# Where the numerator of the time mixing is made: VectorE behind the reciprocal, or GpSimd beside the denominator

## The chip, the cores and the metric

The kernel runs on one core of a Trainium2 chip. It is a single program that computes two transformer layers. The metric is its time on the device in microseconds. The kernel before takes 920.26 us, the median of 3 runs (918.15 to 921.51).

## The reference

There are 8 x 256 tokens of 256 features. Layer 0 is attention followed by a mixture of four experts, layer 1 is an RWKV time mixing followed by a mixture of eight experts. The change lies in the time mixing. Its core is a recurrence over the 256 tokens of a sequence, for each feature apart:

```
def step(carry, kv):
    aa, bb, pp = carry
    kt, vt = kv
    qt = jnp.maximum(pp, kt + u)
    e1 = jnp.exp(pp - qt)
    e2 = jnp.exp(kt + u - qt)
    out = (e1 * aa + e2 * vt) / (e1 * bb + e2)
    pp_new = jnp.maximum(pp + neg_ew, kt)
    f1 = jnp.exp(pp - pp_new)
    f2 = jnp.exp(kt - pp_new)
    return ((f1 * aa + f2 * vt, f1 * bb + f2, pp_new), out)
```

Around it: `k`, `v` and `r` are projections of the token mixed with the one before it, and the output is `r` times the layer norm of `out`, projected by `Wo` and added to the residual:

```
wkv = _wkv(time_decay, time_first, k, v)
mu = jnp.mean(wkv, axis=-1, keepdims=True)
var = jnp.mean(jnp.square(wkv - mu), axis=-1, keepdims=True)
ln = (wkv - mu) * jax.lax.rsqrt(var + LN_EPS) * ln_g + ln_b
rwkv = r * ln
return jnp.einsum('btd,ed->bte', rwkv, Wo)
```

## The kernel before, in words

The program is a chain of phases with a barrier between each two. The time mixing (`rwkv_phase`) is one of them. It makes eight passes, one per sequence `b` of 256 tokens. Features lie on the partitions, in two blocks of 128, and tokens lie along a row, so that almost every elementwise operation is 128 partitions by 512 elements of float32, all in SBUF unless a PSUM bank is named.

Each engine runs through the same hand-written list, `schedule(w)`, and does only the steps that it has; its instructions run in the order of that list. Semaphores, one per kind of result, order the engines among each other: `done["wkv_done"]` counts the passes whose `wkv` is there. Inside an engine an instruction that reads what the one ahead has written waits for its semaphore as well; in `divide` the small helper `then` does both. Several steps of the pass before, `b - 1`, lie between the steps of pass `b`.

The steps of one pass, with the engine and the line:

- `scores`: VectorE makes the running maximum (two scans, L1665), `less` (L1669); ScalarE takes the exponentials (L1631); GpSimd multiplies by `v` (`grow`, L1759). `gap`: VectorE, L1675. `clamp`: ScalarE makes `ex`, which holds e1 and e2 (L1640), GpSimd makes `e2v` (L1763).
- `vary(b - 1)`: TensorE's variance matmuls (L1572), VectorE's small addition (L1716), GpSimd's inverse root (L1768).
- `scan`: VectorE makes `ab`, the sums aa and bb, with four scans of 128x256 (L1682). On GpSimd `scan` is the numerator: e1 times aa (`e1a`, L1772), and its sum with `e2v` (`num`, L1776).
- `gather_up(b + 3)`: GpSimd adds the two expert outputs of a later sequence to the residual (L1743, L1746), after ScalarE has weighed them (`weigh`, L1586). Only the first five passes have it.
- `divide`: VectorE makes the denominator (L1694, L1695), its reciprocal (L1696) and the product with `num` (`wkv`, L1699).
- `add(b - 1)` and `stats(b + 3)` on VectorE; then, in the next pass of the list, `centre(b)` on TensorE (L1545), `square` on ScalarE (L1626), `gate` on VectorE (L1706), `shift`, `add_shift` (L1711) and `project` (L1563).

`products(b + 1)` on TensorE (L1533, 48 matmuls) lies beside `scan` and `divide`.

Of the kernel before, what the change touches and what calls it, by code (L numbers as in the profile page):

```python
# [7 lines left out]
ALU = mybir.AluOpType  # L8
# [6 lines left out]
B, T, D = 8, 256, 256  # L15
# [15 lines left out]
def at_least(eng, semaphore, value):  # L31

    if not (isinstance(value, int) and value <= 0):
        eng.wait_ge(semaphore, value)
# [1361 lines left out]
def rwkv_phase(nc, m, r, k, ctx):  # L1396
# [13 lines left out]
    less, sc, ab = sb("less", [P, 2, EB, T]), sb("sc", [P, 3, EB, T]), sb("ab", [P, 2, EB, T + 1])  # L1410
    dif, rel, ex = sb("dif", [P, EB, T]), sb("rel", [P, 2, EB, T]), sb("ex", [P, 2, EB, T])
    e2v, e1a, num, den, rden, wkv, sq, rw = (
        sb(n, [P, EB, T]) for n in ("e2v", "e1a", "num", "den", "rden", "wkv", "sq", "rw"))
# [6 lines left out]
    done = {n: sem(n) for n in names.split()}  # L1420
# [6 lines left out]
    def schedule(w):  # L1427

        def front(b):
            w.turn(b)  # L1430
            w.take_x(b)

        for b in range(2):
            w.weigh(b)
            w.gather_up(b)
            w.stats(b)
            w.root(b)
            w.norm(b)
            if b == 0:
                front(0)  # L1440
        w.products(0)
        w.weigh(2)
        w.gather_up(2)
        w.stats(2)
        for b in range(B):
            if b + 1 < B:
                front(b + 1)
            if b > 0:
                w.centre(b - 1)
            w.scores(b)  # L1450
            if b > 0:
                w.square(b - 1)
            w.grow(b)
            if b + 2 < B:
                w.root(b + 2)
            w.gap(b)
            if b > 0:
                w.gate(b - 1)
                w.shift(b - 1)
            w.clamp(b)  # L1460
            if b > 0:
                w.add_shift(b - 1)
                w.project(b - 1)
                w.vary(b - 1)
            if b + 2 < B:
                w.norm(b + 2)
            if b + 3 < B:
                w.weigh(b + 3)
            if b + 1 < B:
                w.products(b + 1)  # L1470
            w.scan(b)
            if b + 3 < B:
                w.gather_up(b + 3)
            w.divide(b)
            if b > 0:
                w.add(b - 1)
            if b + 3 < B:
                w.stats(b + 3)
        for step in (w.centre, w.square, w.gate, w.shift, w.add_shift, w.project, w.vary, w.add):
            step(B - 1)  # L1480
# [27 lines left out]
    @block.sync  # L1508
    def _(sp):
        for b in range(B):  # L1510
            for c in range(2):
                plane = k.y_dram[c * TOK + S * P * b:c * TOK + S * P * (b + 1)]
                sp.dma_start(y[:, c, S * b:S * b + S, :], plane.rearrange("(s p) d -> p s d", p=P)).then_inc(here[c][b], 16)
# [132 lines left out]
    def _(dve):  # L1646
        class Dve(Work):
# [38 lines left out]
            def divide(self, b):  # L1686
                def then(ins, name):

                    ins.then_inc(done[name], 1)
                    dve.wait_ge(done[name], b + 1)  # L1690

                dve.wait_ge(done["scan_done"], b + 1)
                dve.wait_ge(done["ex_done"], b + 1)
                then(dve.tensor_tensor(den[:], ex[:, 0], ab[:, 1, :, 0:T], ALU.mult), "e1b_done")  # L1694
                then(dve.tensor_tensor(den[:], den[:], ex[:, 1], ALU.add), "den_done")  # L1695
                then(dve.reciprocal(rden[:], den[:]), "rden_done")  # L1696
                dve.wait_ge(done["num_done"], b + 1)
                at_least(dve, done["centred"], b)
                dve.tensor_tensor(wkv[:], num[:], rden[:], ALU.mult).then_inc(done["wkv_done"], 1)  # L1699

# [36 lines left out]
    @block.gpsimd  # L1737
    def _(pool):
        class Pool(Work):
            def gather_up(self, b):  # L1740
                two = m.x_res[:, S * b:S * b + S, :]
                pool.wait_ge(done["first_weighed"], b + 1)
                pool.tensor_tensor(two, two, y[:, 0, S * b:S * b + S, :], ALU.add).then_inc(done["first_added"], 1)  # L1743
                pool.wait_ge(done["first_added"], b + 1)
                pool.wait_ge(done["second_weighed"], b + 1)
                pool.tensor_tensor(two, two, y[:, 1, S * b:S * b + S, :], ALU.add).then_inc(done["added"], 1)  # L1746

            def root(self, b):
                two = slice(S * b, S * b + S)
                pool.wait_ge(done["ve_in_done"], b + 1)  # L1750
                pool.tensor_tensor(m.rstd[:, two], ve_in[:, two], m.neg_half[:, 0:S], ALU.pow).then_inc(done["root_done"], 1)
                pool.wait_ge(done["root_done"], b + 1)
                pool.tensor_tensor(neg_mean[:, two], less_mean[:, two], m.rstd[:, two], ALU.mult).then_inc(done["neg_mean_ready"], 1)

            def grow(self, b):
                pool.wait_ge(done["sc_done"], b + 1)
                pool.wait_ge(done["v_ready"], b + 1)
                at_least(pool, done["scan_done"], b)
                pool.tensor_tensor(sc[:, 0], sc[:, 1], vs[:], ALU.mult).then_inc(done["f2v_done"], 1)  # L1759

            def clamp(self, b):
                pool.wait_ge(done["ex_done"], b + 1)
                pool.tensor_tensor(e2v[:], ex[:, 1], vs[:], ALU.mult).then_inc(done["e2v_done"], 1)  # L1763

            def vary(self, b):
                pool.wait_ge(done["ve_done"], b + 1)
                at_least(pool, done["x_done"], b)
                pool.tensor_tensor(rstd[:], ve[:], m.neg_half[:, 0:S], ALU.pow).then_inc(done["rstd_done"], 1)  # L1768

            def scan(self, b):  # L1770
                pool.wait_ge(done["scan_done"], b + 1)
                pool.tensor_tensor(e1a[:], ex[:, 0], ab[:, 0, :, 0:T], ALU.mult).then_inc(done["e1a_done"], 1)  # L1772
                pool.wait_ge(done["e1a_done"], b + 1)
                pool.wait_ge(done["e2v_done"], b + 1)
                at_least(pool, done["wkv_done"], b)
                pool.tensor_tensor(num[:], e1a[:], e2v[:], ALU.add).then_inc(done["num_done"], 1)  # L1776

        pool.memset(xt[:, :, :, 0], 0.0)
        pool.memset(top[:, :, 0], NEVER)
        pool.memset(ab[:, :, :, 0], 0.0).then_inc(done["edges"], 1)  # L1780
        schedule(Pool())
        pool.wait_ge(done["eps_done"], 1)
        pool.tensor_tensor(m.rstd[:], m.var_eps[:], m.neg_half[:, 0:NT], ALU.pow).then_inc(done["next_rstd"], 1)
# [86 lines left out]
```

## Time and profile before

| | |
|---|---|
| median of 3 runs | 920.26 us (918.15 to 921.51) |
| profiled execution | 921.07 us |
| its span | 919.3 us |
| busy: TensorE, VectorE | 666.3 us (72%), 541.0 us (59%) |
| busy: ScalarE, GpSimd | 354.4 us (39%), 287.9 us (31%) |
| mean granted TensorE clock | 0.871 of full speed |
| VectorE reciprocals, L1696 | 8, mean 3353 ns |
| VectorE second denominator step, L1695 | 8, mean 1552 ns |
| GpSimd L1772 and L1776 | 8 each, mean 1685 and 1596 ns |

The profile is of one execution. PE is TensorE, PEld its weight loads, DVE VectorE, ACT ScalarE, POOL GpSimd, SP the queue that starts transfers. A row of the timeline gives the start from the beginning of the span, the length, the engine, the line and operation, what it writes and reads, and in brackets how long the engine was idle ahead of it and what released it. The row of a line that occurs several times in a row is merged, with the count at its end. Busy shares over the whole span mix phases of different kinds, so that the stretch of the time mixing has to be read by itself.

### The profile page before, as it was taken

What the parts mean: (1) busy time and instruction counts of PE and PEld (TensorE: products, weight loads), DVE (VectorE), ACT (ScalarE), POOL (GpSimd) and SP (SyncE); (2) the same over time, 40 slices, a digit from 0 to 9 for tenths busy, and PEclk for the clock granted to TensorE, in tenths of its full rate; (3) what the DMA queues carried; (4) which work ended last, traced back from release to release, by engine and by line L of the source; (5) the groups of instructions that cost most, each with busy time, mean ns of one, the idle gap of its engine ahead of it and who ended that gap; (6) DMA issues with size and microseconds to landing.
All of it is one profiled execution on the core that took longest, in us unless ns stands there. A gap on an engine that the chain in (4) does not pass through costs nothing. (4 is left out here: it accounts for less than half of the span.)

```text
span 919.3 us, 14453 instructions
## 1 busy us (share of the span) xinstructions
PE 666.3 (72%) x4496; PEld 560.0 (61%) x4496; DVE 541.0 (59%) x1117; ACT 354.4 (39%) x782; POOL 287.9 (31%) x265
## 2 busy tenths in 40 slices
PE   0389999846971999999963798999507439999800
PEld 0266666526971788888853677888407428888700
DVE  3138787843976455554431588888657755555433
ACT  0048777722531233333323545644104314444300
POOL 3134324010001334433323454552330033332075
PEclk9989999986995899999995989999755559999955
DMA  3000000003520211111105000000025313323144
GB/s 103 16 1 2 2 1 2 2 5 134 183 81 7 86 58 54 57 52 59 52 30 184 0 1 0 1 0 1 0 73 173 125 35 92 93 93 87 53 132 142
DMA packets 38311, 52.20 MB, mean 57 GB/s; under 512 B 7222, under 2 KB 30392, under 8 KB 38232
## 3 DMA queue, kind: packets, MB, share of 16 engines
q1 hardware_dynamic: 31468, 32.74, 11.1%
q0 software_dynamic: 6768, 18.49, 7.0%
q8 instruction: 43, 0.70, 0.3%
q14 instruction: 32, 0.26, 0.1%
HBM read 35.22 MB, written 15.99 MB: 56 GB/s over the span
## 5 line engine op out<-in xcount | busy, mean ns | idle before, releaser
L1533 PE MATMUL banks<-r_xt,r_w_mixed 128*128 128x256 f32 x384 | 86.6, 385 | 3.0 <-ACT r_xt L1601 3.0
L1533 PEld LDWEIGHTS banks<-r_xt,r_w_mixed 128*128 128x128 f32 x384 | 73.2, 192 | 14.0 <-ACT r_xt L1601 3.6
L1299 DVE SCALAR_TENSOR_TENSOR f0x_s<-f0x_th,banks 128x512 f32<-128x512 f32 x35 | 24.1, 689 | 83.3 <-ACT f0x_th L1267 80.8
L614 POOL TENSOR_TENSOR a_rr<-a_ms_eps,neg_half 128x32 f32<-128x32 f32 x8 | 44.0, 5503 | 89.6 <-DVE a_ms_eps L507 89.6
L1176 POOL DMA_INDIRECT f_y<-f0x_yout,f_slot_of x35 | 34.4, 983 | 103.1 <-ACT f0x_yout L1280 101.0
L1162 POOL DMA_INDIRECT f1x_xg<-f_xn,f_token_of x39 | 37.0, 948 | 80.9 <-PE banks L1213 55.4
L1229 PE MATMUL banks<-f_w_hi,f0x_xt_hi 128*128 x140 | 58.9, 420 | 0.2 <-issue 0.2
L534 DVE TENSOR_REDUCE a_ssum<-a_e 128x6 f32<-128x1536 f32 x32 | 55.7, 1742 | 2.3 <-ACT a_e L466 2.3
L1229 PE MATMUL banks<-f_w_lo,f0x_xt_hi 128*128 x140 | 56.0, 400 | 0.0
L1229 PE MATMUL banks<-f_w_hi,f0x_xt_lo 128*128 x140 | 55.6, 397 | 0.0
L1267 ACT ACTIVATE f0x_th<-banks 128x512 f32<-128x512 f32 x35 | 21.0, 599 | 83.8 <-PE banks L1229 83.8
L466 ACT ACTIVATE a_e<-banks 128x1536 f32<-128x1536 f32 x32 | 46.5, 1454 | 12.8 <-PE banks L368 12.8
L1162 POOL DMA_INDIRECT f0x_xg<-f_xn,f_token_of x35 | 33.9, 968 | 30.7 <-POOLq L1809 20.3
L368 PE MATMUL banks<-a_ut,a_qt 32*128 32x256 f32 x512 | 37.6, 408 | 7.8 <-ACT a_e L456 5.6
L1299 DVE SCALAR_TENSOR_TENSOR f1x_s<-f1x_th,banks 128x256 f32<-128x256 f32 x39 | 16.4, 421 | 45.0 <-ACT f1x_th L1267 44.3
L1250 PE MATMUL banks<-f_w_hi,f0x_ht_hi 128*128 x140 | 42.4, 303 | 0.7 <-ACT f0x_yout L1280 0.7
L1356 POOL DMA_INDIRECT f1c_y<-f_y,f_row_of x32 | 30.3, 946 | 38.7 <-PEq L1806 29.3
L1250 PE MATMUL banks<-f_w_lo,f0x_ht_hi 128*128 x140 | 39.5, 282 | 0.0
L1250 PE MATMUL banks<-f_w_hi,f0x_ht_lo 128*128 x140 | 39.4, 281 | 0.0
L393 PE MATMUL banks<-a_e,a_vv 128*32 128x256 f32 x512 | 34.3, 385 | 3.4 <-DVE a_vv L549 2.7
L368 PEld LDWEIGHTS banks<-a_ut,a_qt 32*128 32x128 f32 x512 | 24.0, 188 | 19.6 <-issue 12.9
L1366 DVE SCALAR_TENSOR_TENSOR x_res<-f1c_y,f_weight,x_res 128x256 f32<-128x256 f32 x32 | 15.5, 484 | 32.5 <-DMA f1c_y<-f_y,f_row_of 30.3
(362 smaller groups left out, 2034.1 us busy)
## 6 DMA issues: line engine op xcount, KB each, us to landing
f_y<-f1x_yout SPq DMA_DIRECT2D x39, 128.0 KB, 1.7
f0r_stage<-in_f_w13T SPq DMA_DIRECT2D x4, 1024.0 KB
r_y<-f_y SPq DMA_DIRECT2D x16, 256.0 KB, 5.7
f1r_stage<-in_f_w13T SPq DMA_DIRECT2D x8, 512.0 KB, 5.3
x_res<-in_L_attn_x SPq DMA_DIRECT2D x2, 1024.0 KB
f0r_stage<-in_f_w2T SPq DMA_DIRECT2D x4, 512.0 KB
f_xn<-f0r_xn SPq DMA_DIRECT2D x8, 256.0 KB
f1r_stage<-in_f_w2T SPq DMA_DIRECT2D x8, 256.0 KB, 5.4
```

The costliest lines, as they stand in the source:

```text
L368: last = pe.matmul(scores[:, i, s, :], qt[rows, b % 2, e, k, s * P:(s + 1) * P], ut[rows, b % 2, k, :], start=True, stop=True)
L393: last = pe.matmul(av(n)[32 * i:32 * i + 32, :], values[:, b % 2, head, :, :].rearrange("p r d -> p (r d)"), side[:, S * i + s, :], start= ...
L466: act.activation(ebuf[:, n % 3, 0:SUMS_ON_DVE, :], scores[:, 0:SUMS_ON_DVE // S].rearrange("p i s t -> p (i s) t"), ACT.Exp).then_inc(exp_ ...
L534: dve.tensor_reduce(ssum[:, b % 2, NB * p:NB * p + SUMS_ON_DVE], ebuf[:, n % 3, 0:SUMS_ON_DVE, :], AX_X, ALU.add).then_inc(sum_done, 1)
L614: pool.tensor_tensor(rr[:], ms_eps[:], m.neg_half[:, 0:S * NH], ALU.pow).then_inc(rr_found, 1)
L1162: pool.indirect_dma_start(xg[:, t % GB, :], None, k.xn_dram, bass.IndirectOffsetOnAxis(ap=k.token_of[:, t:t + 1], axis=0)).then_inc(gather ...
L1176: pool.indirect_dma_start(k.y_dram, bass.IndirectOffsetOnAxis(ap=k.slot_of[:, t:t + 1], axis=0), yout[:, t % YB, :], None).then_inc(scatte ...
L1229: last = pe.matmul(out, xt[a][:, t % 2, kb * P:(kb + 1) * P], k.w13[c][kb][:, e, cols], start=(i == 0 and not v.lin_bias), stop=(i == len( ...
L1250: last = pe.matmul(y_psum, ht[a][:, t % 2, hb * P:(hb + 1) * P], k.w2[c][hb][:, e, :], start=(i == 0 and not v.lin_bias), stop=(i == len(s ...
L1299: dve.scalar_tensor_tensor(out=s1[:, t % 2, :], in0=th[:, t % 2, :], scalar=1.0, in1=glu(t), op0=ALU.add, op1=ALU.mult).then_inc(s1_done, 1)
L1356: pool.indirect_dma_start(y[:, t % GB, c, :], None, k.y_dram, bass.IndirectOffsetOnAxis(ap=k.row_of[:, c * NT + t:c * NT + t + 1], axis=0) ...
L1533: last = pe.matmul(bank(1 + kind)[:, eb * T:(eb + 1) * T], r.w_mixed[:, kind, j // KB, j % KB, eb * P:(eb + 1) * P], xt[:, b % 2, j % KB, ...
```

## The change

VectorE makes the numerator itself. In `divide`, behind the reciprocal, two instructions are added: `e1a` = e1 times aa, and `num` = `e1a` + `e2v`. The wait for `num_done` becomes a wait for `e2v_done`. GpSimd's `scan` step is taken away with its two instructions and its waits. The semaphores keep their names and counts.

```diff
--- before.py
+++ after.py
@@ -1694,7 +1694,9 @@
                 then(dve.tensor_tensor(den[:], ex[:, 0], ab[:, 1, :, 0:T], ALU.mult), "e1b_done")
                 then(dve.tensor_tensor(den[:], den[:], ex[:, 1], ALU.add), "den_done")
                 then(dve.reciprocal(rden[:], den[:]), "rden_done")
-                dve.wait_ge(done["num_done"], b + 1)
+                then(dve.tensor_tensor(e1a[:], ex[:, 0], ab[:, 0, :, 0:T], ALU.mult), "e1a_done")
+                dve.wait_ge(done["e2v_done"], b + 1)
+                then(dve.tensor_tensor(num[:], e1a[:], e2v[:], ALU.add), "num_done")
                 at_least(dve, done["centred"], b)
                 dve.tensor_tensor(wkv[:], num[:], rden[:], ALU.mult).then_inc(done["wkv_done"], 1)
 
@@ -1767,13 +1769,6 @@
                 at_least(pool, done["x_done"], b)
                 pool.tensor_tensor(rstd[:], ve[:], m.neg_half[:, 0:S], ALU.pow).then_inc(done["rstd_done"], 1)
 
-            def scan(self, b):
-                pool.wait_ge(done["scan_done"], b + 1)
-                pool.tensor_tensor(e1a[:], ex[:, 0], ab[:, 0, :, 0:T], ALU.mult).then_inc(done["e1a_done"], 1)
-                pool.wait_ge(done["e1a_done"], b + 1)
-                pool.wait_ge(done["e2v_done"], b + 1)
-                at_least(pool, done["wkv_done"], b)
-                pool.tensor_tensor(num[:], e1a[:], e2v[:], ALU.add).then_inc(done["num_done"], 1)
 
         pool.memset(xt[:, :, :, 0], 0.0)
         pool.memset(top[:, :, 0], NEVER)
```

On VectorE, the second pass, from the four scans of `scan` (L1682, called SCALAR_TENSOR_TENSOR here and TENSOR_TENSOR_SCAN in the trace) to `add` (`x_res`, and its BN_STATS). `r_ex` holds e1 and e2, `r_ab` aa and bb. Before:

```order
L1682 SCALAR_TENSOR_TENSOR r_ab<-r_sc 128x256 x4
L1694 TENSOR_TENSOR r_den<-r_ex,r_ab 128x512
L1695 TENSOR_TENSOR r_den<-r_den,r_ex 128x512
L1696 RECIPROCAL r_rden<-r_den 128x512
L1699 TENSOR_TENSOR r_wkv<-r_num,r_rden 128x512
L1724 SCALAR_TENSOR_TENSOR x_res<-banks,r_rstd,x_res 128x256 x2
L1729 BN_STATS bn<-x_res 128x6 x2
```

After:

```order
L1682 SCALAR_TENSOR_TENSOR r_ab<-r_sc 128x256 x4
L1694 TENSOR_TENSOR r_den<-r_ex,r_ab 128x512
L1695 TENSOR_TENSOR r_den<-r_den,r_ex 128x512
L1696 RECIPROCAL r_rden<-r_den 128x512
L1697 TENSOR_TENSOR r_e1a<-r_ex,r_ab 128x512
L1699 TENSOR_TENSOR r_num<-r_e1a,r_e2v 128x512
L1701 TENSOR_TENSOR r_wkv<-r_num,r_rden 128x512
L1726 SCALAR_TENSOR_TENSOR x_res<-banks,r_rstd,x_res 128x256 x2
L1731 BN_STATS bn<-x_res 128x6 x2
```

Two instructions of 128x512 stand between the reciprocal and the product with it; everything behind them in the queue is two places later.

On GpSimd, from `r_e2v` of the second pass to `grow` (`r_sc`) of the third and the root for a later norm (`rstd`). The root of the variance is L1768 before and L1770 after, the two additions of the gather are L1743 and L1746 before, L1745 and L1748 after. Before:

```order
L1763 TENSOR_TENSOR r_e2v<-r_ex,r_vs 128x512
L1768 TENSOR_TENSOR r_rstd<-r_ve,neg_half 128x2
L1772 TENSOR_TENSOR r_e1a<-r_ex,r_ab 128x512
L1776 TENSOR_TENSOR r_num<-r_e1a,r_e2v 128x512
L1743 TENSOR_TENSOR x_res<-x_res,r_y 128x512
L1746 TENSOR_TENSOR x_res<-x_res,r_y 128x512
L1759 TENSOR_TENSOR r_sc<-r_sc,r_vs 128x512
L1751 TENSOR_TENSOR rstd<-r_ve_in,neg_half 128x2
```

After:

```order
L1765 TENSOR_TENSOR r_e2v<-r_ex,r_vs 128x512
L1770 TENSOR_TENSOR r_rstd<-r_ve,neg_half 128x2
L1745 TENSOR_TENSOR x_res<-x_res,r_y 128x512
L1748 TENSOR_TENSOR x_res<-x_res,r_y 128x512
L1761 TENSOR_TENSOR r_sc<-r_sc,r_vs 128x512
L1753 TENSOR_TENSOR rstd<-r_ve_in,neg_half 128x2
L1755 TENSOR_TENSOR r_neg_mean<-r_less_mean,rstd 128x2
```

The two additions of the gather move up: they follow the root of the variance directly.

## Rows read from the trace of the kernel before

The columns of rows 1 and 6 are: the stretch, its length, then busy time and number of instructions of PE, PEld, DVE, ACT and POOL (of PE alone in rows 6), the granted TensorE clock as a part of full speed, the busy share of the DMA engines, and GB/s.

**Rows 1.** Busy time by stretch, the first and the third pass; columns named above.

```profile
520.00:539.00 19.00, 12.42 (x52) 10.40 (x50) 15.40 (x20) 11.58 (x21) 12.02 (x12) 0.82 0.00 0
...
557.90:576.60 18.70, 17.18 (x85) 14.87 (x85) 16.15 (x26) 10.09 (x19) 10.20 (x10) 1.00 0.01 1
```

**Rows 2.** Waits from 515 to 675 us: total, times, longest.

```profile
DVE r_ve L1716 <- PE banks L1572: 17.3, 8, 2.3
...
PE banks L1545 <- DVE r_wkv L1699: 15.9, 2, 9.3
...
DVE r_rw L1706 <- PE banks L1545: 3.0, 1, 3.0
```

**Rows 3.** Timeline of the third pass, all engines: start, length, instruction, idle before.

```profile
557.71 10.62 PE L1533 MATMUL banks<-r_xt,r_w_mixed 128*128 128x256 f32 x48
557.89 0.16 DVE L1716 TENSOR_SCALAR r_ve<-banks 128x2 f32<-128x2 f32 x1 [2.28 <-PE banks L1572]
557.97 2.74 DVE L1682 TENSOR_TENSOR_SCAN r_ab<-r_sc 128x256 f32<-128x256 f32 x4
558.22 1.69 ACT L1586 ACTIVATE r_y<-r_y,f_weight 128x256 f32<-128x256 f32 x4
558.37 1.07 POOL L1768 TENSOR_TENSOR r_rstd<-r_ve,neg_half 128x2 f32<-128x2 f32 x1
560.74 0.69 DVE L1694 TENSOR_TENSOR r_den<-r_ex,r_ab 128x512 f32<-128x512 f32 x1
560.78 1.69 POOL L1772 TENSOR_TENSOR r_e1a<-r_ex,r_ab 128x512 f32<-128x512 f32 x1 [1.33 <-DVE r_ab L1682]
...
561.46 1.55 DVE L1695 TENSOR_TENSOR r_den<-r_den,r_ex 128x512 f32<-128x512 f32 x1
...
562.55 1.60 POOL L1776 TENSOR_TENSOR r_num<-r_e1a,r_e2v 128x512 f32<-128x512 f32 x1
563.05 3.35 DVE L1696 RECIPROCAL r_rden<-r_den 128x512 f32<-128x512 f32 x1
564.11 1.27 POOL L1743 TENSOR_TENSOR x_res<-x_res,r_y 128x512 f32<-128x512 f32 x1
...
565.45 1.27 POOL L1746 TENSOR_TENSOR x_res<-x_res,r_y 128x512 f32<-128x512 f32 x1
566.44 0.83 DVE L1699 TENSOR_TENSOR r_wkv<-r_num,r_rden 128x512 f32<-128x512 f32 x1
...
568.61 0.60 PE L1545 MATMUL banks<-r_wkv,r_cen_same 128*128 128x256 f32 x2
...
570.54 0.60 ACT L1626 ACTIVATE r_sq<-banks 128x512 f32<-128x512 f32 x1 [1.08 <-PE banks L1545]
...
573.01 0.68 DVE L1706 TENSOR_TENSOR r_rw<-banks,r_s 128x512 f32<-128x512 f32 x1
...
573.75 1.99 PE L1563 MATMUL banks<-r_wo_gain,r_rw 128*128 128x256 f32 x8 [1.52 <-DVE r_rw L1706]
...
576.56 0.16 DVE L1716 TENSOR_SCALAR r_ve<-banks 128x2 f32<-128x2 f32 x1 [2.28 <-PE banks L1572]
```

**Rows 4.** Timeline of the first pass.

```profile
520.79 3.46 DVE L1682 TENSOR_TENSOR_SCAN r_ab<-r_sc 128x256 f32<-128x256 f32 x4 [1.88 <-POOL r_sc L1759]
...
522.01 1.70 POOL L1763 TENSOR_TENSOR r_e2v<-r_ex,r_vs 128x512 f32<-128x512 f32 x1
```

**Rows 5.** Single lines: ns least/median/most, first and last start.

```profile
L1682 DVE TENSOR_TENSOR_SCAN r_ab<-r_sc x32: 656/659/1691, 520.8 to 650.7; 128x256 f32<-128x256 f32 x32
...
L1694 DVE TENSOR_TENSOR r_den<-r_ex,r_ab x8: 691/692/693, 524.3 to 651.3; 128x512 f32<-128x512 f32 x8
...
L1695 DVE TENSOR_TENSOR r_den<-r_den,r_ex x8: 1549/1552/1555, 525.0 to 652.1; 128x512 f32<-128x512 f32 x8
...
L1699 DVE TENSOR_TENSOR r_wkv<-r_num,r_rden x8: 691/816/836, 530.0 to 657.0; 128x512 f32<-128x512 f32 x8
```

**Rows 6.** Busy time by stretch, TensorE alone, in the attention phase.

```profile
172.00:184.00 12.00, 9.89 (x126) 1.00 0.00 1
```

## The prediction

> **What bounds the kernel now.** Only one of the kernel's phases is touched, the time mixing, whose eight passes over pairs of 128-token tiles fill about 520 to 670 us. I first read the busy time by stretch, one stretch per pass. In the third pass VectorE is busy for 16.15 of 18.70 us and TensorE for 17.18, so either could be the bound, and the shares do not say which [rows 1]. The waits of the phase do. VectorE has one wait that returns in every pass: 17.3 us in 8 times, at most 2.3 each, at the small addition that starts a pass (L1716), for TensorE's variance matmuls (L1572) [rows 2]. The timeline of the third pass closes the loop. VectorE starts L1716 at 557.89 and has no other wait until the gate product L1706 ends at 573.69 (573.01 + 0.68); TensorE, which had stood 1.52 us for exactly that product, starts the projection at 573.75, its variance matmuls follow, and VectorE goes on with the next L1716 at 576.56 [rows 3]. The period of 18.67 us is thus 15.8 us of VectorE's queue plus 2.87 us of TensorE behind it. Everything that lengthens VectorE's queue lengthens the pass by as much. TensorE starts the centring (L1545) only at 568.61, though its input r_wkv is there from 567.27 (566.44 + 0.83): it has 1.3 us in hand at that place and another 1.52 before the projection [rows 3]. In the first and the last pass it has nothing in hand: two waits of 15.9 us together for r_wkv, and the last pass's gate waits 3.0 us for the centring [rows 2]. So the result of the division is on the path in all eight passes: through VectorE's own queue in the first seven, through TensorE's wait in the last.
>
> GpSimd's decayed product and sum (L1772, L1776) are not on it. The sum ends at 564.15 (562.55 + 1.60), inside the reciprocal, which runs from 563.05 to 566.40 [rows 3]. What they cost today is interference. L1695 adds two SBUF tensors of the same size as L1694 and takes 1549 to 1555 ns in all 8 passes, against 691 to 693 for L1694 [rows 5]; the difference of 0.86 us stands where GpSimd's L1772 is running, itself 1.69 us long where the same kind of operation in L1743 takes 1.27 [rows 3]. L1699, too, takes 0.83 us while L1746 is still running until 566.72 and a least 0.69 us elsewhere [rows 3, 5]. So an operation of either engine with two SBUF inputs is held up until the other's is through. The reciprocal, with one input, shows no such thing: 3.35 us with two and a half GpSimd operations beside it [rows 3].
>
> **The change part by part.**
>
> *Added on VectorE.* Two 128x512 products per pass, behind the reciprocal and each waited for before the next goes. The first is L1694's form, the second L1695's. The pitch from L1694 to L1695, the wait for completion included, is 561.46 - 560.74 = 0.72 us [rows 3]. 8 x 2 x 0.72 = +11.5 us, all on the path. The wait for e2v in front of the sum costs nothing: e2v is GpSimd's operation before L1768, which starts at 558.37 [rows 3], and the sum comes eight microseconds later.
>
> *Removed: the interference with L1695 and L1699.* If nothing took the place of GpSimd's two operations, L1695 would fall to 0.69: 8 x 0.86 = -6.9 us. L1699 would be 0.69 in all passes; it is longer by 0.12 to 0.14 in the five passes that still gather (median 816, least 691) [rows 5]: 5 x 0.14 = -0.7 us.
>
> *Moved: the gathers.* GpSimd's queue is in order, and with the two operations gone its next ones after the root L1768 are the two additions of the gather for three passes on (L1743, L1746), in the first five passes. Today they run from 564.11 to 566.72, under the reciprocal, where they meet only the start of L1699. After the change they wait for nothing but ScalarE's weighing L1586: four instructions in the 1.69 us from 558.22, the first two done by about 559.1 [rows 3]. L1768 ends at 559.45, so L1743 starts at about 559.50, amid VectorE's four scans (557.97 to 560.71), which also read two SBUF inputs. What such a meeting costs is seen in the first pass: GpSimd's L1763 starts at 522.01 within the four scans and takes 1.70 instead of 1.27, and the four scans take 3.46 us [rows 4]; the longest scan of all is 1691 ns where the median is 659 [rows 5]. The meeting costs VectorE 1.03 us. By the same steps L1743 is held until about 559.9, ends at 561.2 and puts the last scan off by 1.03. L1746 then starts at about 561.3 behind the last scan's reads and stands before L1694, which it puts off by as much again. I take 1.03 for both, the row nearest to what they meet: 5 x 2 x 1.03 = +10.3 us. The bounds of one meeting are 0 (they happen to fall between VectorE's operations) and 1.27 (the whole of L1743): 0 to 12.7 in all. L1695, after them, is free in all eight passes, as counted.
>
> By the Trainium skill ("SBUF — State Buffer", section "Who interferes with whom") whoever comes first has the shared ports for the whole instruction and the other stops entirely, which would make a meeting worth up to the whole gather addition; with 1.27 for 1.03 the sum would be 2.4 us more. The 1.03 us of [rows 5] is below that, and I keep the row's value.
>
> *Sum.* 11.5 - 6.9 - 0.7 + 10.3 = +14.2 us: about +2.5 in each of the first five passes, +0.58 (1.44 - 0.86) in each of the last three. The profiled execution took 921.07 us, of which 919.3 are span; it would go to 935.3. It lies 0.8 above the median of 920.26, to which I add the same 14.2: **934.5 us**.
>
> *What is late next.* With r_wkv 2.5 us later in the middle passes, TensorE's 1.3 us in hand at the centring is gone and it starts 1.2 us later. The squares (L1626) that follow start at 570.54, and the gate that wants them at 573.01, itself 2.5 later: they stay ahead [rows 3]. TensorE then idles about 4 of 21.2 us per pass.
>
> **The rivals.**
>
> *A. The gathers hit less than I say.* They are put off by ScalarE or slip between two operations, so that about one meeting per pass is paid instead of two: 14.2 - 5.2 = +9.0, 929.3 us. For it: the start at 559.50 lies within about 0.1 us of the third scan's own start, if the scans (0.66 us each, four in 2.74) start some 0.6 us apart, so small shifts change who goes first. Against it: GpSimd's 2.6 us of gathers starting at 559.5 cannot avoid the stretch to 562 in which VectorE reads two tensors almost without pause. If both meetings were free, 14.2 - 10.3 = +3.9, 924.2 us; this needs the order of GpSimd's queue not to matter at all.
>
> *B. TensorE's clock falls.* With more idle time per pass, the granted clock, now 1.00 in the third pass and 0.82 in the first, where TensorE stood for r_wkv [rows 1, 2], could drop to the lower level for part of a pass. In the first pass TensorE is busy 12.42 of 19 us. If the projection and the variance behind it (2.87 us) ran at 1.2 GHz instead of 2.4, that is up to +2.9 us per pass for seven passes, +20: 954 us, and the products, 10.62 us at full clock [rows 3], would come near to bounding the pass. Against it: at 172 to 184 us it is busy 9.89 of 12.00, 82%, with the clock at 1.00 [rows 6], and the pass after the change would have 17.2 of 21.2, 81%.
>
> *C. Not slower: the loop closes through TensorE.* If TensorE, with 17.18 of 18.70 us busy, set the pass, then six of eight passes would swallow VectorE's additions up to the 1.3 us in hand at L1545 and the 1.52 at L1563, and only the first and last pass would pay: +2.5 + 0.6 = +3.1 at most, 923.3 us, or nothing if the earlier gathers help the next norm. It decides if VectorE's addition is under what TensorE has in hand and the 2.3 us wait at L1716 shrinks by it. Against it: that wait is behind TensorE's wait for L1706, so it cannot shrink when L1706 comes later.
>
> **How the numbers follow.** The forecast (both meetings paid, loop through VectorE) 0.63; A 0.15 for one meeting and 0.09 for none; B 0.07; C 0.04, with another 0.02 for a gain that I have no mechanism for. The likeliest case is 934.5. The range reaches down to A's first case and up past the dearer meeting, 927 to 940, leaving out B and the cases of 924 and less. What a measurement of this kernel can tell from no change is about 0.5%, 4.6 us, so 924.9 is the line of slower. Slower: 0.63 + 0.15 + 0.07 and a little of A's second case, 0.86; within 0.5%: the rest of A and C, 0.12; faster 0.02.
>
> **What would show it.** Right: L1695 at 0.69 in all passes; the two new VectorE lines at 0.69 each with a pitch of 0.72; a last scan of about 1.7 us and an L1694 of about 1.7 us in five passes, with the gather additions beside them; a period of about 21.2 us in passes two to five and 17.9 in six and seven; VectorE's wait at L1716 still 2.3 us; TensorE waiting more for r_wkv. Wrong: gathers that still run beside the reciprocal or scans of 0.66 throughout (A); a granted clock under 1.00 in passes two to seven (B); a shrinking wait before the variance addition (C).

## The result and the profile after

The changed kernel takes 937.38 us, the median of 4 runs (936.2 to 938.35), against 919.88 us for the kernel before, also of 4. The ratio is 1.019, with a 95% interval of 1.0168 to 1.0212: slower by 17.5 us where +14.2 was forecast, and inside the range. The profiled execution has a span of 936.6 us and a mean granted clock of 0.858.

The same view as in [rows 1], from one small variance addition (L1718, L1716 before) to the next: the stretch, its length, busy time of PE, PEld, DVE, ACT and POOL, granted clock, DMA share, GB/s.

```profile
541.30:564.37 23.07, 19.02 (x85) 16.19 (x85) 18.84 (x27) 11.86 (x24) 7.88 (x8) 0.92 0.00 1
...
585.10:606.37 21.27, 17.41 (x85) 14.87 (x85) 18.65 (x27) 10.08 (x19) 7.17 (x8) 1.00 0.00 0
606.37:629.30 22.93, 19.08 (x85) 16.22 (x85) 18.66 (x28) 10.51 (x19) 7.71 (x8) 0.92 0.00 1
```

The fourth pass, between 585 and 606, is as forecast: 21.27 us long with the clock at 1.00, against 18.70 in [rows 1]. The two others shown, the second and the fifth, are 1.8 and 1.7 us longer still, at a clock of 0.92. The fourth pass in the timeline (start, length, instruction, idle before), to be read against [rows 3]:

```profile
585.10 0.16 DVE L1718 TENSOR_SCALAR r_ve<-banks 128x2 f32<-128x2 f32 x1 [2.28 <-PE banks L1572]
585.18 4.89 DVE L1682 TENSOR_TENSOR_SCAN r_ab<-r_sc 128x256 f32<-128x256 f32 x4
...
585.59 1.08 POOL L1770 TENSOR_TENSOR r_rstd<-r_ve,neg_half 128x2 f32<-128x2 f32 x1
586.64 1.27 POOL L1745 TENSOR_TENSOR x_res<-x_res,r_y 128x512 f32<-128x512 f32 x1
587.99 1.53 POOL L1748 TENSOR_TENSOR x_res<-x_res,r_y 128x512 f32<-128x512 f32 x1
...
590.10 0.69 DVE L1694 TENSOR_TENSOR r_den<-r_ex,r_ab 128x512 f32<-128x512 f32 x1
590.83 0.69 DVE L1695 TENSOR_TENSOR r_den<-r_den,r_ex 128x512 f32<-128x512 f32 x1
591.55 3.35 DVE L1696 RECIPROCAL r_rden<-r_den 128x512 f32<-128x512 f32 x1
...
594.94 0.69 DVE L1697 TENSOR_TENSOR r_e1a<-r_ex,r_ab 128x512 f32<-128x512 f32 x1
...
595.66 0.69 DVE L1699 TENSOR_TENSOR r_num<-r_e1a,r_e2v 128x512 f32<-128x512 f32 x1
...
596.39 0.69 DVE L1701 TENSOR_TENSOR r_wkv<-r_num,r_rden 128x512 f32<-128x512 f32 x1
...
597.14 0.70 PE L1545 MATMUL banks<-r_wkv,r_cen_same 128*128 128x256 f32 x2 [1.16 <-DVE r_wkv L1701]
...
602.82 0.68 DVE L1708 TENSOR_TENSOR r_rw<-banks,r_s 128x512 f32<-128x512 f32 x1
...
603.56 1.99 PE L1563 MATMUL banks<-r_wo_gain,r_rw 128*128 128x256 f32 x8 [2.70 <-DVE r_rw L1708]
...
606.37 0.16 DVE L1718 TENSOR_SCALAR r_ve<-banks 128x2 f32<-128x2 f32 x1 [2.28 <-PE banks L1572]
```

The numerator's product and sum stand behind the reciprocal with pitches of 0.72 and 0.73 us. L1695 takes 0.69 us where it took 1.55. The gather additions L1745 and L1748 run at 586.64 and 587.99, amid the scans, and the four scans take 4.89 us instead of 2.74. VectorE has no wait from L1718 to the gate product L1708; TensorE stands 1.16 us for r_wkv and 2.70 for L1708, which it did for 0 and 1.52 before. VectorE's own wait is again 2.28.

The single lines over all passes, as in [rows 5] (ns least, median, most):

```profile
L1682 DVE TENSOR_TENSOR_SCAN r_ab<-r_sc x32: 656/680/1775, 520.8 to 668.2; 128x256 f32<-128x256 f32 x32
...
L1694 DVE TENSOR_TENSOR r_den<-r_ex,r_ab x8: 691/692/1583, 524.3 to 668.8; 128x512 f32<-128x512 f32 x8
...
L1695 DVE TENSOR_TENSOR r_den<-r_den,r_ex x8: 691/692/1640, 525.9 to 669.6; 128x512 f32<-128x512 f32 x8
...
L1748 POOL TENSOR_TENSOR x_res<-x_res,r_y x8: 1254/1531/1592, 490.1 to 609.3; 128x512 f32<-128x512 f32 x8
```

L1694 is long in the first and the third pass and L1695 in the first; in the second, fourth and fifth both gather additions fall among the scans. The waits of the phase, as in [rows 2] (total, times, longest):

```profile
PE banks L1545 <- DVE r_wkv L1701: 20.8, 5, 9.9
DVE r_ve L1718 <- PE banks L1572: 20.1, 8, 3.9
...
PE banks L1563 <- DVE r_rw L1708: 11.4, 5, 2.7
```

VectorE waits 20.1 us instead of 17.3 for the variance, at most 3.9. The pass that ends with the 3.89 us shows why:

```profile
553.53 0.70 PE L1545 MATMUL banks<-r_wkv,r_cen_same 128*128 128x256 f32 x2 [1.35 <-DVE r_wkv L1701]
...
559.95 2.89 PE L1563 MATMUL banks<-r_wo_gain,r_rw 128*128 128x256 f32 x8 [2.70 <-DVE r_rw L1708]
...
562.63 1.70 PE L1572 MATMUL banks<-r_mean_of,r_sq 128*128 128x1 f32 x8
...
564.37 0.16 DVE L1718 TENSOR_SCALAR r_ve<-banks 128x2 f32<-128x2 f32 x1 [3.89 <-PE banks L1572]
564.45 3.46 DVE L1682 TENSOR_TENSOR_SCAN r_ab<-r_sc 128x256 f32<-128x256 f32 x4
...
565.60 1.76 POOL L1745 TENSOR_TENSOR x_res<-x_res,r_y 128x512 f32<-128x512 f32 x1
567.44 1.53 POOL L1748 TENSOR_TENSOR x_res<-x_res,r_y 128x512 f32<-128x512 f32 x1
567.95 1.57 DVE L1694 TENSOR_TENSOR r_den<-r_ex,r_ab 128x512 f32<-128x512 f32 x1
```

TensorE had stood for r_wkv and again for the gate product, and then took 2.89 us for a projection that takes 1.99, and 1.70 for variance matmuls that took 0.95 at full clock. By the profile the granted clock was 1.00 until 560 us and 0.50 from 561 to 567 us, the lower of its two levels (2.4 and 1.2 GHz). What TensorE did before it fell was to stand those 1.35 and 2.70 us.

### The profile page after: what moved, and what is told of

Same layout as the page of the kernel before. It is cut to its first block and busy times, and to the rows that moved or that the text cites. A ratio compares the mean times of both kernels' runs of the same rounds, so it can differ in the third digit from the quotient of the medians.

```text
span 936.6 us, 14452 instructions
## 1 busy us (share of the span) xinstructions
PE 676.3 (72%) x4496; PEld 567.6 (61%) x4496; DVE 555.3 (59%) x1133; ACT 354.1 (38%) x782; POOL 263.6 (28%) x249
## 5 line engine op out<-in xcount | busy, mean ns | idle before, releaser
L1533 PE MATMUL banks<-r_xt,r_w_mixed 128*128 128x256 f32 x384 | 93.0, 405 | 3.0 <-ACT r_xt L1601 3.0
L1533 PEld LDWEIGHTS banks<-r_xt,r_w_mixed 128*128 128x128 f32 x384 | 77.9, 205 | 15.8 <-ACT r_xt L1601 3.6
L1761 POOL TENSOR_TENSOR r_sc<-r_sc,r_vs 128x512 f32<-128x512 f32 x8 | 10.2, 1276 | 99.8 <-ACT r_sc L1631 99.8
```

The costliest lines, as they stand in the source:

```text
L1533: last = pe.matmul(bank(1 + kind)[:, eb * T:(eb + 1) * T], r.w_mixed[:, kind, j // KB, j % KB, eb * P:(eb + 1) * P], xt[:, b % 2, j % KB, ...
```

## The experiments

Where a kernel is compared with another than the one before, both ratios to the kernel before are used, since each group of runs had its own runs of that kernel (medians of 920.56 to 921.36 us).

**e1: the gathers back under the reciprocal**

```diff
     pool.wait_ge(done["first_weighed"], b + 1)
+    at_least(pool, done["den_done"], b - 2)
     pool.tensor_tensor(two, two, y[:, 0, S * b:S * b + S, :], ALU.add).then_inc(done["first_added"], 1)
```

> The changed kernel, with GpSimd's first gather addition (L1745 there) of the first five passes also waiting for the denominator of its pass, so that both additions run beside the reciprocal again, as before the change. Theory, that the moved gathers cost what they hold up in VectorE's scans and denominator (in the third pass of the changed kernel 3.46 - 2.74 us in the scans and 1.57 - 0.69 in L1694, 1.6 together; up to 2.5 in the second): five passes give back 8 to 10 us, 937.4 to about 928.5 (927 to 930), all scans near 0.66 us, L1694 and L1695 both at 0.69 in all eight passes. Rival 1, that only the two products added to VectorE count and the place of the gathers does not: no change, 937 (936 to 938.5). Rival 2, that the clock of TensorE is the larger part of what lies beyond 11.5 us: the gathers' delay gives back under 4 us, 933.5 or more.

Measured: 926.88 us, ratio 1.0059 (1.0043 to 1.0076). The place of the gathers alone is worth 1.019 - 1.0059 = 0.013, 12 us, somewhat more than the 8 to 10 expected. The two denominator lines, all eight passes:

```profile
L1694 DVE TENSOR_TENSOR r_den<-r_ex,r_ab x8: 692/692/692, 525.3 to 657.6; 128x512 f32<-128x512 f32 x8
...
L1695 DVE TENSOR_TENSOR r_den<-r_den,r_ex x8: 691/692/693, 526.0 to 658.4; 128x512 f32<-128x512 f32 x8
```

The terms that are left, 11.5 - 6.9 - 0.7 = +3.9, would give 1.0042. One wait for the variance in this trace is 4.0 us, 1.7 more than the usual 2.3; with it the sum is +5.6, and 0.0059 of 921.2 is 5.4. Rivals 1 and 2 are out. The expectation counted VectorE's lengths alone and left out the clock, and the changed kernel has two such long waits where e1 has one. That this is all of the 2 to 4 us by which it was missed is not shown.

**e8: only one of the two additions meets VectorE**

```diff
     pool.wait_ge(done["second_weighed"], b + 1)
+    at_least(pool, done["den_done"], b - 2)
     pool.tensor_tensor(two, two, y[:, 1, S * b:S * b + S, :], ALU.add).then_inc(done["added"], 1)
```

> The changed kernel, with only the second gather addition (L1748 there) waiting for the denominator, so that in the first five passes one of the two meets VectorE's scans and the other runs beside the reciprocal. Theory, that each meeting costs VectorE about 1 us: between e1 (none, 1.006 of before) and the changed kernel (both, 1.019), five us above e1: a ratio of 1.0115 (1.010 to 1.013), about 932. Rival, that only the pair costs, by making TensorE's clock fall: near e1, under 1.009, or near the changed kernel, over 1.016.

Measured: 932.64 us, ratio 1.0122 (1.0101 to 1.0143), halfway as expected. The third pass, and the end of it:

```profile
561.04 3.86 DVE L1682 TENSOR_TENSOR_SCAN r_ab<-r_sc 128x256 f32<-128x256 f32 x4
...
583.71 0.16 DVE L1718 TENSOR_SCALAR r_ve<-banks 128x2 f32<-128x2 f32 x1 [4.78 <-PE banks L1572]
```

The scans take 3.86 us, 1.1 more than the 2.74 of before. The clock takes part here too: the wait that ends this pass is 4.78 us, and the execution that was profiled is the slowest of the six (929.41 to 936.0 us). So the halfway ratio is not a clean price of one meeting; the length of the scans is.

**e2: the two operations alone, added to the kernel before**

The lines that declare the two tiles and their semaphores are left out here.

```diff
     then(dve.reciprocal(rden[:], den[:]), "rden_done")
+    then(dve.tensor_tensor(more1[:], ex[:, 0], ab[:, 0, :, 0:T], ALU.mult), "more1_done")
+    then(dve.tensor_tensor(more2[:], more1[:], ex[:, 1], ALU.add), "more2_done")
```

> The kernel before, with two further 128x512 operations of the same forms (e1 times aa, and a sum with e2) on VectorE behind the reciprocal, written to tiles that nobody reads; GpSimd makes the numerator as before. It measures the first term of the sum alone. Theory, that VectorE's queue sets the period of every pass: 8 x 2 x 0.72 = +11.5 us, 919.9 to 931.4 (930 to 934 with some clock loss), L1695 still at 1.55 us in all passes. Rival, that the loop closes through TensorE: at most +3.1, under 923.5.

Measured: 935.08 us, ratio 1.015 (1.0131 to 1.0169), or +13.9. The rival, a loop that closes through TensorE, is out. But 13.9 is 2.4 more than 11.5, and the product with the reciprocal, 0.69 us in every pass of this trace, should have given 0.7 back. The wait for the variance (total, times, longest) tells where a part of it lies, in the slowest of the five executions (939.0 us):

```profile
DVE r_ve L1719 <- PE banks L1573: 20.8, 8, 4.8
```

**e10: e2 with filler matmuls**

TensorE gets work that nobody reads in the place where it stands for the gate product, in passes two to six. The two operations of e2 are in it as well; their lines are left out here.

```diff
     last.then_inc(done["shifted"], 1)
+    if 1 <= b <= 5:
+        at_least(pe, done["ve_done"], b)
+        for n in range(4 if b < 5 else 3):
+            pe.matmul(bank(5)[:, T:2 * T], m.ident[:], r.wo_shift[:, n % EB, :], start=True, stop=True)
```

> The kernel of e2 (before, with two more 128x512 operations on VectorE per pass) with four filler matmuls behind the shift product of the second to the fifth pass, three in the sixth. Theory, that e2's excess over 11.5 us is TensorE's clock: no low stretch in passes two to six, VectorE's wait for the variance 2.3 at most, 11.5 - 0.7 = 10.8 us above before, a ratio of 1.012 (1.0105 to 1.0135) against e2's 1.015. Rival, that two more operations cost more than their own pitch elsewhere: the same 1.015.

Measured: 931.69 us, ratio 1.0115 (1.0094 to 1.0136), or +10.6. Doing more on TensorE made the kernel shorter by 0.0035; the two intervals overlap by a little (this one ends at 1.0136, e2's starts at 1.0131), so the ratios alone leave room, but the view agrees:

```profile
DVE r_ve L1723 <- PE banks L1577: 17.3, 8, 2.3
```

Total and longest are again those of [rows 2]. With the clock kept up, the first term less the 0.7 us of the product with the reciprocal, 10.8 us, is thus measured as 10.6.

**e4: eight fillers in every pass of the changed kernel**

The edit of e10, without the condition on `b` and with eight matmuls.

> The changed kernel, with eight matmuls of 128x256 by constants into an unused part of a PSUM bank behind the shift product of each pass, where TensorE stands 1.5 to 2.7 us for VectorE's gate product. They only keep TensorE busy. Theory, that about 3 us of the 17.5 come from the granted clock, which is at 0.5 for two stretches of 6.8 us in the third and the sixth pass and makes VectorE wait 3.9 instead of 2.3 us for the variance matmuls: no such stretch in passes two to seven, VectorE's wait 2.3 at most, 937.4 to about 934.5 (933 to 936). Rival, that these stretches come from elsewhere or cost nothing: 937 or more, slower still if the fillers (1.9 us at full clock) hold up the projection in the passes where the wait is shorter.

Measured: 946.67 us, ratio 1.0274 (1.0255 to 1.0293): slower than the changed kernel by 0.0073 to 0.0084, 7 to 8 us, against the theory's number and as its rival warned. The fillers were mis-sized: each is 0.43 us, eight take 3.45, not 1.9. In the pass after the last gather (TensorE alone):

```profile
644.25 3.62 PE L1559 MATMUL banks<-r_wo_shift,ident 128*128 128x256 f32 x16
647.70 1.89 PE L1566 MATMUL banks<-r_wo_gain,r_rw 128*128 128x256 f32 x8
```

The projection (L1566) starts right behind the fillers (L1559), with no idle time for the gate product. The four passes that begin at 545, 566, 588 and 609 us are nonetheless 21.23 us each, all alike, with the granted clock at 1.00, where the changed kernel has 23.07, 20.73, 21.27 and 22.93: 3.1 us less together. The loss lies in the first pass (4.4 us) and the last three (7.1 together), by the starts of the variance addition. The run shows that the low stretches go with TensorE's idle time, and does not price them.

**e6: four fillers in four passes**

The edit of e10 with `if 1 <= b <= 4` and four matmuls, on the changed kernel.

> The changed kernel, with four filler matmuls (0.43 us each by e4's trace, 1.7 together) instead of eight, and only behind the shift product of the second to the fifth pass, where TensorE stands 1.8 to 2.7 us for the gate product. Theory, that the low clock in the third and sixth pass costs about 3 us: the fillers fit into the wait, the clock stays at 1.00 there, VectorE's wait for the variance is 2.3 at most, 937.4 to about 934.5 (933 to 935.5). Rival 1, that the clock's share is nothing: 937 or more. Rival 2, that four do not keep it up: the same low stretches, 937 to 938.

Measured: 933.36 us, ratio 1.0138 (1.0121 to 1.0156). This interval lies clear of the changed kernel's in both of its measurements (1.019, and 1.0201 in e9). The third pass of e6 by stretch, columns as above, then its wait for the variance, and then the sixth pass of the changed kernel:

```profile
561.50:582.80 21.30, 19.17 (x93) 16.41 (x93) 18.68 (x28) 10.10 (x19) 7.20 (x8) 1.00 0.00 1
```

```profile
DVE r_ve L1722 <- PE banks L1576: 17.3, 8, 2.3
```

```profile
629.30:647.89 18.59, 18.59 (x85) 16.08 (x86) 15.25 (x22) 7.27 (x12) 2.81 (x3) 0.91 0.00 1
```

The clock is 1.00 in e6, the wait 2.3 at most. The clock is worth 0.0052 to 0.0063, 5 to 6 us; the theory's 3 was too low. It counted the two longer waits alone (3.89 and 3.93 instead of 2.28 us, 3.3 together). But the second low stretch reaches into the sixth pass, where TensorE is then busy for all of 18.59 us; the sixth and seventh pass take 18.59 and 18.15 us, against 17.94 and 17.88 in e6, 0.9 more. What is left, 0.0138 or 12.7 us, is the change without its clock loss: the meetings with the gathers, worked out as under "The moved gathers" below, cost VectorE 10.2 us here, as good as the changed kernel's 10.3.

**e7: the kernel before, again, and e9: the changed kernel, again**

> The kernel before once more, for a second trace. The traces of the changed kernel and of e1 to e3 have 13.6 us for the first 24 products of the time mixing, that of before 12.2, with the granted clock at 0.5 for 23.9 and 20.5 us around it. Theory, that this belongs to the single trace and not to the change: here 13.6 us too, or the low stretch placed otherwise, and the phase 1 to 1.5 us longer than 187.8; passes two to seven with the periods of the first trace (18.4 to 18.7 and 17.3) and the clock at 1.00. Rival, that it comes from the change: 12.2 us and 187.8 again.

Measured: 922.21 us, one run. The phase takes 190.4 us here, not 187.8, which is more than the 1 to 1.5 us expected, and the first 24 products, 48 records in the trace, take about as long as the 13.6 us in the changed kernel's trace:

```profile
497.27 13.67 PE L1533 MATMUL banks<-r_xt,r_w_mixed 128*128 128x256 f32 x48 [0.69 <-ACT r_xt L1601]
```

In the first trace they took 12.2 us. So what the opening of the phase takes differs by over a microsecond between two executions of one kernel, and a difference of that kind between the traces of before and after is not the change's. From the third pass on the periods are the first trace's within 0.01 us (18.67, 18.69, 18.68, 17.33, 17.29) with the clock at 1.00 in the passes of [rows 1]'s kind.

> The changed kernel once more, on the chip of the next run, so that the kernels of the study can be set against it, and for a second trace. Theory: a ratio of 1.017 to 1.021 to the kernel before; in the first five passes one or two operations of VectorE with two SBUF inputs longer by 0.7 to 1.1 us each for a gather addition; one to three stretches of the lower TensorE clock within passes two to seven, not all at the places of the first trace. Rival, that the two stretches are fixed by the program: again in the third and the sixth pass, 6.8 us each.

Measured: 939.29 us, ratio 1.0201 (1.0178 to 1.0223). The waits for the variance are again long at the start of the third and the sixth pass (3.84 and 3.85 us), and the scans again take 3.46 us in the third pass and 4.89 in the fourth and fifth. The rival expectation holds: the low stretches are where they were, within 0.5 us. The theory's guess that they would move did not come true.

**e3: the numerator stays on GpSimd, but under the reciprocal**

```diff
     pool.wait_ge(done["scan_done"], b + 1)
+    pool.wait_ge(done["den_done"], b + 1)
     pool.tensor_tensor(e1a[:], ex[:, 0], ab[:, 0, :, 0:T], ALU.mult).then_inc(done["e1a_done"], 1)
```

> The kernel before, with GpSimd's first numerator product (L1772 there) waiting for the finished denominator, so that both its operations run beside the reciprocal and not beside L1694 and L1695. Theory, that the interference of 0.86 us per pass at L1695 is a matter of place alone: L1695 falls to 0.69 in all passes, the numerator (2 x 1.34 us) is there before the reciprocal's 3.35 us are over, and the first gather addition, which then starts just ahead of the product with the reciprocal (L1699), holds that up by 0.2 to 0.5 in five passes: -6.9 + 1 to 2, 919.9 to about 914.5 (913 to 916). Rival, that the numerator comes too late or that the interference moves along with it: the same time or slower, 920 to 924.

Measured: 916.54 us, ratio 0.9949 (0.9932 to 0.9966). One more wait on the kernel before makes it faster, by 4.7 us, a little less than the 5 to 6 expected:

```profile
579.55 0.69 DVE L1695 TENSOR_TENSOR r_den<-r_den,r_ex 128x512 f32<-128x512 f32 x1
...
580.27 3.35 DVE L1696 RECIPROCAL r_rden<-r_den 128x512 f32<-128x512 f32 x1
580.38 1.18 POOL L1773 TENSOR_TENSOR r_e1a<-r_ex,r_ab 128x512 f32<-128x512 f32 x1 [2.85 <-DVE r_den L1695]
581.64 1.27 POOL L1777 TENSOR_TENSOR r_num<-r_e1a,r_e2v 128x512 f32<-128x512 f32 x1
582.87 1.27 POOL L1743 TENSOR_TENSOR x_res<-x_res,r_y 128x512 f32<-128x512 f32 x1
...
583.66 1.03 DVE L1699 TENSOR_TENSOR r_wkv<-r_num,r_rden 128x512 f32<-128x512 f32 x1
```

L1695 is free, both numerator operations end before the reciprocal does at 583.62, and the first gather addition holds L1699 up to 1.03 us, 0.2 more than before. The passes with gathers are 0.65 us shorter for it, and the sixth and seventh, which have none, only 0.44 and 0.59.

**e5: e3, with the statistics in VectorE's wait**

The edit against e3:

```diff
-            if b + 2 < B:
-                w.root(b + 2)
+            if b == 0:
+                w.root(2)
...
                 w.add_shift(b - 1)
+                if b + 2 < B:
+                    w.stats(b + 2)
+                    w.root(b + 2)
                 w.project(b - 1)
                 w.vary(b - 1)
...
-            if b + 3 < B:
-                w.stats(b + 3)
...
                 pool.wait_ge(done["first_weighed"], b + 1)
+                at_least(pool, done["wkv_done"], b - 2)
```

> The kernel with the numerator on GpSimd under the reciprocal (e3), and two moves more: the gather additions of the first five passes wait for r_wkv, and the statistics of the gathered tiles (four short VectorE operations, some 1.3 us) go to where VectorE stands 2.28 us for the variance matmuls, with the root for them on GpSimd behind e2v. Theory, that VectorE's queue up to the gate product is what counts: it loses 1.3 us and the collision of L1699 (1.03 instead of 0.69), but TensorE, which stands only 0.86 us before the projection in e3, becomes the bound, so that a pass gains 0.86 and not 1.6: five passes 4 us, 916.5 to about 912.5 (911 to 914). Rival, that the statistics hold up the variance addition or the norm comes too late for the next transposes: 916 or slower.

Measured: 912.15 us, ratio 0.9911 (0.9894 to 0.9928), the fastest kernel of the study. One pass in the timeline, and by stretch:

```profile
579.77 0.69 DVE L1700 TENSOR_TENSOR r_wkv<-r_num,r_rden 128x512 f32<-128x512 f32 x1
...
581.96 2.29 DVE L1666 TENSOR_TENSOR_SCAN r_kt<-r_grown,r_kt 128x256 f32<-128x256 f32 x2
581.96 1.74 POOL L1748 TENSOR_TENSOR x_res<-x_res,r_y 128x512 f32<-128x512 f32 x1
...
586.02 0.68 DVE L1707 TENSOR_TENSOR r_rw<-banks,r_s 128x512 f32<-128x512 f32 x1
...
586.76 1.99 PE L1564 MATMUL banks<-r_wo_gain,r_rw 128*128 128x256 f32 x8 [0.31 <-DVE r_rw L1707]
...
589.58 0.16 DVE L1717 TENSOR_SCALAR r_ve<-banks 128x2 f32<-128x2 f32 x1 [1.06 <-PE banks L1573]
```

```profile
572.20:589.60 17.40, 17.09 (x85) 14.78 (x85) 16.07 (x26) 9.97 (x18) 10.67 (x10) 1.00 0.00 0
```

TensorE is busy 17.09 of 17.40 us, but it still stands 0.31 for the gate product, and VectorE has no wait between L1717 and that product. So VectorE's queue still sets the pass, with TensorE 0.31 us behind it. From one L1717 to the next it is 17.47 us, against 18.02 in e3. VectorE's queue lost 1.20 us of statistics and 0.34 at L1700, but the second gather addition, moved once more, now meets the two scans of the running maximum (L1666), which take 2.29 us instead of e3's 1.26. That leaves 0.5 of the 1.5 us. The expectation, 912.5, was hit by luck: it put the smaller gain down to TensorE as the new bound, and the trace shows a new meeting.

## Why the prediction was right

*The bound.* VectorE's queue up to the gate product sets the period. e2 and e10 show it alone: two operations of 0.72 us per pass lengthen the kernel by +13.9 and, with the clock kept up, +10.6 us (8.7 to 12.5), where the first term was 11.5, less the 0.7 of the product with the reciprocal, which is free there too. Rival C is out. The period of 21.2 us came out in the fourth pass (21.27), and the 17.9 us of the sixth and seventh in e6 (17.94, 17.88); in the changed kernel itself, behind the second low stretch, they are 18.59 and 18.15.

*Freed interference.* L1695 is at 0.69 us wherever no gather addition meets it, as forecast. e3 takes the same 0.86 us off L1695 in each pass without moving any work to another engine, and 4.7 of these 6.9 us reach the kernel's time.

*The moved gathers.* This is the step that the diff does not show, and it decided the size. Against the lengths of before, the meetings cost VectorE in the first five passes 1.84, 2.58, 1.61, 2.14 and 2.15 us: (1.58 - 0.69) + (1.64 - 0.69) in the first, 3.46 - 2.74 + 1.57 - 0.69 in the third, and the longer scans alone in the other three (5.08 - 2.50, 4.89 - 2.75 and 4.89 - 2.74). The sum is 10.3 us, the value that was forecast. That it agrees so closely is in part luck: I had put one meeting in the scans and one at L1694 in every pass, and this was so in the third alone, and the five costs lie between 1.61 and 2.58 where I had 2.06 for each. By the Trainium skill ("SBUF — State Buffer", "Who interferes with whom") the shared ports are an exclusive lock and the later one is stopped for the whole instruction, which would be up to 2.54 for two additions. The page has the words on the whole instruction beside VectorE's two-port modes; of an operation with two SBUF inputs it says only that it contends with GpSimd's reads. One pass of five reaches 2.54, the mean is 2.06. e1 takes the meetings away, e8 one of the two.

*Rival B, TensorE's clock.* It was set against the forecast as another case, at 954 us, and it came true beside it in small. I had argued that TensorE would keep 1.00 since it was as busy elsewhere at that clock; that argument failed. Low stretches across the start of the third and the sixth pass make two waits 1.6 us longer, and behind the second the sixth and seventh pass are together 0.9 us longer than in e6. e6, which differs from the changed kernel by fillers alone, prices it at 5 to 6 us. This is what the sum of 14.2 lacks against 17.5; without it e6 measures 12.7 (11.1 to 14.4). So the sum of 14.2 was by 1.5 us too high, which is within e6's interval, and the term that it put at nothing, the clock, made up for that and more.

*Rival A* has no case in the traces: the additions met VectorE twice in all five passes.

What stays open is why the low stretches come at those two passes and not at others with the same idle time. The fillers show that the low stretches go away when TensorE's idle time is filled, not which part of it brings them.

## What to carry to other kernels

Taking operations from an in-order queue moves up everything behind them. Ask what the next ones will run beside: here two gather additions left the cover of a one-input reciprocal for four two-input scans, and cost about as much as the work that was moved. In e5 one of them moved again and met two other scans. Before moving work between VectorE and GpSimd because they interfere, try a wait that puts it beside an operation that does not interfere (e3, one line, 0.5% faster). And where VectorE's queue, which sets the period, grows, look at TensorE's granted clock per pass, since its new idle time can have a price of its own.

## What the runs showed of the hardware

- An operation with two SBUF inputs on VectorE and one on GpSimd delay each other: at 512 elements per partition VectorE lost 0.7 to 1.3 us in a full meeting (0.72 in the scans of the third pass, 2.58 for two in the second) and 0.1 to 0.3 where it met only the end (L1699: 0.83 and 1.03 instead of 0.69 us), GpSimd 0.3 to 0.5 (1.53 to 1.76 instead of 1.27); the reciprocal, with one input, stays at 3.35 us beside any of them.
- The lower clock came back at the same two passes in two executions of the changed kernel, and work of no use, 1.7 us on TensorE in each of four passes (e6), made the kernel 5 to 6 us faster.
- The opening 24 products of the same kernel took 12.2 us in one execution, at a mean granted clock of 0.87, and 13.7 in another, at 0.77.
